# The search of a quantised feed-forward block on one core: running maxima and minima on VectorE in place of a maximum pass and a copy on ScalarE

## The reference

```
x = x + attention(layernorm(x), ctx, Wq, Wkv)
x = x + ffn(layernorm(x), w_gate, w_up, w_down)
```

```
def act_qdq(x):
    scale = max(max(abs(x)) / 32767, 1e-12)
    return clip(round(x / scale), -32768, 32767) * scale
x    = act_qdq(x)
up   = act_qdq(x @ lpbq_dequant(w_up).T)
gate = act_qdq(x @ lpbq_dequant(w_gate).T)
sig  = fixed_qdq_u16(sigmoid(gate))
gate = act_qdq(gate * sig)
o    = act_qdq(gate * up)
return o @ lpbq_dequant(w_down).T
```

## Time and profile before

| what | value |
|---|---|
| three executions | 890.88, 889.6, 889.14 us |
| profiled execution, its own time | 889.12 us |
| its span, first to last instruction | 887.3 us |
| TensorE busy | 858.3 us, 97% |
| VectorE busy | 689.5 us, 78% |
| ScalarE busy | 585.5 us, 66% |
| mean granted TensorE clock | 0.994 of full |

### The profile page before, as it was taken

The page is one execution under the profiler, slowest core; times in us unless marked ns, Lnnn a source line. Parts: engine busy times, 40 slices in busy tenths (PEclk is TensorE's granted clock), DMA queues, the critical chain, the costliest instruction groups (busy, mean ns, idle before and its releaser), DMA issues.

```text
span 887.3 us, 11953 instructions
## 1 busy us (share of the span) xinstructions
PE 858.3 (97%) x4108; PEld 424.5 (48%) x4108; DVE 689.5 (78%) x965; ACT 585.5 (66%) x712; POOL 195.4 (22%) x170
## 2 busy tenths in 40 slices
PE   7999969999999999999999999999899989999998
PEld 5877544444444444444444444444444434444443
DVE  4879885566647459689998987584999997999892
ACT  2468776785655366599999987752889965455430
POOL 0099948399300295000000000000000000000000
PEclk9999989999999999999999999999999999999999
DMA  9822228766989549999779964997998887989872
GB/s 348 339 84 109 107 83 288 232 169 188 304 252 313 196 156 238 270 379 371 261 258 341 334 236 161 357 378 262 323 406 271 277 319 273 374 299 401 316 294 96
DMA packets 118402, 236.56 MB, mean 267 GB/s; under 512 B 47952, under 2 KB 57168, under 8 KB 116304
## 3 DMA queue, kind: packets, MB, share of 16 engines
q1 hardware_dynamic: 117200, 231.77, 74.0%
q10 hardware_dynamic: 1152, 4.19, 1.2%
HBM read 130.55 MB, written 95.42 MB: 255 GB/s over the span
## 4 chain that ended last, share of the span: by engine, by line
PE 71%; DVE 9%; POOL 8%; issue 6%; DMA 3%; SPq 1%; ACT 1%; DVEq 0%; ACTq 0%; POOLq 0%
PE ps L1106 28%; PE ps L1043 21%; PE ps L1159 13%; PE ps L1059 4%; PE ps L1186 4%; DVE big L1960 3%; DVE big L1953 3%; POOL big L875 2%; DMA big<-in_L_ffn_w_gate_dram 2%; POOL big L832 1%; POOL big L826 1%; PE ps L1176 1%; POOL small L872 1%; DMA big<-up_park 1%; POOL big L830 1%
## 5 line engine op out<-in xcount | busy, mean ns | idle before, releaser
L1106 PE MATMUL ps<-big 128*128 (+1 forms) x1152 | 248.8, 379 | 0.0
L1204 ACT ACTIVATE big<-ps 128x1024 f32<-128x1024 f32 (+2 forms) x154 | 126.4, 830 | 147.7 <-PE ps L1043 62.5
L1043 PE MATMUL ps<-big 128*128 (+1 forms) x864 | 186.6, 379 | 0.7 <-DVE big L1736 0.7
L1106 PEld LDWEIGHTS ps<-big 128*128 128x128 f16 x1152 | 112.7, 98 | 135.9
L1043 PEld LDWEIGHTS ps<-big 128*128 128x128 f16 x864 | 84.4, 98 | 102.7 <-issue 0.9
L1159 PE MATMUL ps<-big 128*128 128x512 f16 x576 | 125.1, 379 | 3.2 <-DVE big L1981 3.2
L817 POOL PARTITION_ALL_REDUCE small<-small x8 | 2.9, 368 | 451.6 <-DVE small L1922 170.1
L1781 DVE TENSOR_REDUCE small<-big 128x1 f32<-128x1024 f32 x36 | 43.8, 1218 | 71.0 <-ACT big L1204 71.0
L1159 PEld LDWEIGHTS ps<-big 128*128 128x128 f16 x576 | 56.2, 98 | 71.6 <-issue 2.9
L1140 PE MATMUL ps<-big 128*128 128x512 f16 x384 | 84.2, 379 | 4.3 <-ACT big L1489 4.3
L1874 DVE TENSOR_REDUCE small<-big 128x1 f32<-128x1024 f32 x48 | 58.2, 1215 | 13.7 <-ACT big L1204 13.6
(11 more groups left out here) (118 smaller groups left out, 1222.3 us busy)
## 6 DMA issues: line engine op xcount, KB each, us to landing
big<-up_park SPq DMA_DIRECT2D x90, 512.0 KB, 6.7
big<-gate_park SPq DMA_DIRECT2D x48, 512.0 KB, 6.3
up_park<-big SPq DMA_DIRECT2D x48, 512.0 KB, 4.1
gate_park<-big SPq DMA_DIRECT2D x36, 512.0 KB, 2.7
sign_park<-big SPq DMA_DIRECT2D x36, 256.0 KB, 2.7
big<-in_x_dram SPq DMA_DIRECT2D x8, 1024.0 KB, 18.5
x_park<-big SPq DMA_DIRECT2D x8, 1024.0 KB, 3.9
product_park<-big SPq DMA_DIRECT2D x16, 512.0 KB, 3.5
```

Source lines behind the costliest of these rows:

```text
L1043: mm = nc.tensor.matmul(unit_banks(n)[:, j], WG[:, x, a, k % 2, o:o + P], XT[:, g, b, k], start=(k == 0 and a + b == 0), stop=(k == KC - 1 ...
L1106: mm = nc.tensor.matmul(ps[:, b + j], WU[:, a, t // 3, k, t % 3], XT[:, g, c, k], start=(k == 0 and a + c == 0), stop=(k == KC - 1 and c = ...
L1204: return nc.scalar.activation(dst, src, ACT.Copy)
```

## The change

In the search the split unit's plain product and its maximum pass (two VectorE instructions) are replaced by two other VectorE instructions. The first is the product with a running maximum, the same form of instruction as the whole unit has. The second reads the f32 product and writes the half-precision copy, and accumulates a running minimum of it. VectorE itself waits between the two, and for the place of the copy. ScalarE's `product_hi` is gone. All products are scaled by 2^-15, and `quant_scale` takes this back. The largest absolute value is now that of the maxima and minima, in 50 columns instead of 26.

```
-            nc.scalar.activation(halves[:, PART[t]], seat(2 * t), ACT.Copy, scale=D1_SCALE).then_inc(ph_d, 1)
...
-                product_hi(t)
...
-                nc.vector.tensor_tensor(at, r_int[:, 2 * t % 4], Q[:, HALF[split(t)]], ALU.mult).then_inc(pr_d, 1)
-                dve.wait_ge(pr_d, t + 1)
-                nc.vector.tensor_reduce(ocol[:, 2 + t:3 + t], at, AX.X, ALU.max, apply_absolute_value=True).then_inc(o_mx, 1)
+                top, low = ocol[:, 2 + t:3 + t], ocol[:, 2 + NS + t:3 + NS + t]
+                nc.vector.tensor_tensor_reduce(at, r_int[:, 2 * t % 4], Q[:, HALF[split(t)]], D1_SCALE, top,
+                                               ALU.mult, ALU.max, top).then_inc(o_mx, 1)
+                dve.wait_ge(o_mx, 2 * t + 1)
+                if t in PART_AFTER:
+                    slot_free(dve, PART_AFTER[t])
+                nc.vector.tensor_scalar(halves[:, PART[t]], at, 1.0, FLT_MAX, ALU.mult, ALU.min, low).then_inc(ph_d, 1)
...
-                nc.vector.tensor_tensor_reduce(seat(c), r_int[:, c % 4], Q[:, HALF[whole(t)]], 1.0,
+                nc.vector.tensor_tensor_reduce(seat(c), r_int[:, c % 4], Q[:, HALF[whole(t)]], D1_SCALE,
...
             dve.wait_ge(o_mx, NU)
-            nc.vector.tensor_reduce(col["omx"], ocol, AX.X, ALU.max).then_inc(col_max, 1)
+            dve.wait_ge(ph_d, NS)
+            nc.vector.tensor_reduce(col["omx"], ocol, AX.X, ALU.max, apply_absolute_value=True).then_inc(col_max, 1)
...
-            linked(quant_scale("osc", "oinv", "ot", "orc", "oall", col["oo"]))
+            linked(quant_scale("osc", "oinv", "ot", "orc", "oall", col["oo"], 1.0 / D1_SCALE))
```

More of the change, by code:

```diff
@@ L119 @@
 D1_SCALE = 2.0 ** -15
+FLT_MAX = 3.0e38
 RING = 4
@@ L340, in build @@
         scol = cut(1640, 2)
-        ocol = cut(1688, 2 + NS)
+        ocol = cut(1642, 2 + 2 * NS)
         sc = cut(1736, 64)
@@ L398, in build @@
         sgn_ld = [sem(f"sgn_ld{s}") for s in range(4)]
-        sgn_d, pr_d, ph_d = sem("sgn_d"), sem("pr_d"), sem("ph_d")
+        sgn_d, ph_d = sem("sgn_d"), sem("ph_d")
         d1_mm, d1_ev, d1_use = sem("d1_mm"), sem("d1_ev"), sem("d1_use")
@@ L1712, in _, with quant_scale @@
                     h_max(PAIR_AT[n])
-            def quant_scale(scale, inv, tmp, rec, whole, factor):
-                scalar2(col[tmp], col[whole], factor, 1.0 / QMAX)
+            def quant_scale(scale, inv, tmp, rec, whole, factor, unit=1.0):
+                scalar2(col[tmp], col[whole], factor, unit / QMAX)
                 scalar2(col[scale], col[tmp], TINY, None, ALU.max, ALU.bypass)
```

## The result

The changed kernel takes 892.23 us (median of six executions, 891.72 to 893.83) against 889.37 us beside it. The ratio is 1.0034, with a 95% interval from 1.0021 to 1.0047: it is 0.34% slower, some 2.9 us. The profiled execution has a span of 889.9 us against 887.3 and a time of its own of 891.72 us.

What follows compares the result with a forecast made beforehand. VectorE was taken to bound the search, and TensorE nearly everything else. The split product's longer wait, 24 x (1.31 - 1.25) = +1.4 us, other terms nothing, on 889.6 us gave 891.0 us, range 889.0 to 893.2.

Steps and rivals of the forecast that it cites:

- no change: Whole kernel: time stays within 0.2% of the kernel before's 889.6 us; chance 0.45.
- rival 1: Search: VectorE's copy takes 1276 to 1285 ns or leaves an extra gap; +3.0 us, 892.6 us; chance 0.25.
- What bounds the search: Search: VectorE sets the end, about 3.6 us for each of 24 steps, and all 1.4 us lost arrive.
- ScalarE's 24 copies: Search: ScalarE loses 25.1 us of busy time beside VectorE's work, off the chain; counted as nothing.
- Price of the copy: Search, VectorE's second pass: tensor_scalar with accumulator taken at 1220 ns, next start after 1.13 us, so +0.
- the term of the split product: Search, VectorE: dependent successor starts 1.31 us behind the new product instead of 1.25; 24 steps give +1.4 us.
- The two other distances: Search, VectorE: next start 1.13 us behind the second pass and 1.20 behind the whole product, both +0.
- TensorE's tail stays hidden: End of search: TensorE's last matmuls end at about 715.6 us, before the down projection starts at 718.6.
- Rival 2: Search: the copy runs at 687 ns, TensorE becomes the bound; 5.2 us faster, 884.4 us, or about 887; chance 0.15.
- Rival 3: End of search: an earlier `fetch_u(4)` covers the loss, so nothing reaches the end; 889.6 us; chance 0.07.

Runs made afterwards that it cites:

- e1_product: Kernel before with only the split unit's product changed to the form with a running maximum, ScalarE keeping its copies; ratio 1.0018 to the kernel before.
- e4_order: Changed kernel with VectorE's copy moved behind the whole unit's product of the same step; ratio 0.9992 to the kernel before.
- e5_plain: Changed kernel with the minimum left out of the copy, a plain tensor_scalar; smallest split products left out of the search; ratio 0.9933 to the kernel before.
- e3_warm: Changed kernel with ten extra TensorE matmuls between the first passes and the down projection; ratio 1.0017 to the kernel before.
- e11_warm_again: Changed kernel with the same ten extra TensorE matmuls before the down projection, repeated on another chip; ratio 1.0025 to the kernel before.
- e2_copy: Changed kernel with the plain split product, the copy with minimum staying on VectorE; largest positive split product left out; ratio 0.9998 to the kernel before.
- e8_changed: The changed kernel measured once more, nothing altered; ratio 1.0033 to the kernel before.

## Why the prediction came out as it did

The time, 892.2 us, lies in the range, but 1.2 us above the value given and outside the forecast's own range of 890.4 to 891.8. The change is slower by more than 0.2% where "no change" had the larger chance (0.45 against 0.38). The mechanism of the search was right; that the time fell into the whole range is in part luck, because rival 1, which doesn't occur, had stretched it upwards.

- **What bounds the search.** Right: VectorE sets its end, and what it loses arrives. e1_product and e4_order move the time the way they move VectorE's step, and e5_plain does so down to TensorE's pace. ScalarE's 24 copies were worth nothing, as said.
- **Price of the copy.** Right, 1220 ns, from the rule that what reduces along the row belongs to the slow family and that constants cost less than a per-partition operand. No run tests the second half of that rule by itself. The Trainium skill, SBUF — State Buffer, section Who interferes with whom, leaves the form that writes out its accumulator out of the two-port modes; the traces agree that it is the slow one, 1220 against 694 ns. The Trainium skill, VectorE: DVE Perf Modes, section The perf-mode tier table, gives tensor_scalar on f32 twice the rate; that fits the plain form alone, with its 694 ns.
- **Mis-sized: the term of the split product.** The sum said 24 x 0.06 = 1.4 us, the search grew by 2.0. Averaged over the 24 steps, the successor that waits starts 1.324 us behind this product against 1.255 before, 1.66 us in all. The two other distances, put at nothing, grew as well: behind the copy 1.146 against 1.137 behind the maximum pass, and behind the whole unit's product 1.205 against 1.200, 0.34 us together. Each is about the rounding of the rows that the terms were made from, but 24 steps multiply it.
- **Missing: TensorE's clock.** The prediction said that TensorE's tail stays hidden. That was right for its work and left out its idle time. The prediction's own figures, matmuls that end at 715.6 and a down projection that starts at 718.6, leave 3.0 us idle, and yet it expected TensorE's wait there "as before" (2.41). The first passes follow VectorE's pace more closely now, so TensorE finishes 2.44 us behind the search instead of 2.93, and the 5.35 us to the down projection leave 2.90 us idle instead of 2.41. In the profiles with 2.88 to 2.90 us the first matmuls that follow run at the lower level (four of four); in the seven others with 2.63 us or less they don't. The rest is 176.2 to 176.3 us in the first and 174.8 to 175.5 us in the second, apart from e5_plain; the means of the two groups are 1.15 us apart. That the fall goes with the idle time is what e3_warm and e11_warm_again show by filling it. The length of the idle time isn't the whole rule, though. Ahead of the search TensorE stands idle for 2.46 us, runs 24 small matmuls and stands idle again, and there the clock falls to half in all twelve profiles, in the kernel before too. Its timeline row and two of its stretches (columns as in those of TensorE above):

```profile
622.74 3.48 PE L1088 MATMUL ps<-small 128*96 128x96 f32 x24 [2.46 <-DVE small L1874]
```

```profile
622.00:625.00 3.00, 2.26 (x18) 0.75 0.91 257
625.00:628.00 3.00, 1.22 (x8) 0.69 1.07 358
```

- **The rivals.** Rival 1 had the right size, 892.6 us, for a reason that didn't hold: its 1276 ns or extra gap aren't there. Rival 2 was priced rightly, as e5_plain shows, and doesn't occur. Rival 3 doesn't either: the fifth up tile's load is issued at the end of the search as before.

Open is the exact share of the clock in the mean of many executions: the profiles say 0.8 to 1.3 us, the timed pairs 1.1 with intervals of about one on each side, and e2_copy shows a profile with the fall and a ratio without a loss.

## What to carry to other kernels

When one instruction is exchanged for another on the engine that sets the pace, price the distance to the next start and not the duration, once for a successor that waits and once for one that doesn't. Behind the same product the one that waits came 0.12 us later. The kernel before paid that too, and reordering (e4_order) won back more than the change had cost. Take such distances to a hundredth, because the loop multiplies them. And look at the idle time of TensorE between two phases as well as at its work: half a microsecond more of it went with a fall of the clock that cost about 1 us.

## What was not expected of the hardware

- tensor_scalar from f32 to f16 on 128x1024 takes 694 ns, with an accumulated minimum 1220 ns, under the name TENSOR_SCALAR_CACHE_REDUCE.
- The same product (1.28 us) passes to an independent successor after 1.20 us and to one that waits for it after 1.32. The Trainium skill, VectorE: DVE Perf Modes, section The DRAIN you can't avoid, reports for a chain of eight copies that a semaphore after each costs nothing extra. Here taking the wait away gained 24 x 0.12 us, and for this kernel the measurement decides.
- At the start of the search the clock was at half until 634 us in the changed kernel's profile and full from 628 us on in that of e8_changed; both needed 88.06 and 88.05 us for the first passes, since TensorE has 0.2 us a step in hand to catch up (16 matmuls take 3.47 of the 3.68 us). The same fall behind the search, or at the start of the gate projection, where TensorE has nothing in hand, costs time.
